# State-space layer: the out-projection weights are loaded at the top of each group, for the first group in the head

## The reference

```python
proj = hidden_states @ in_proj_w.T                     # 512 -> 8192 gate, 10240 xBC, 128 dt
xBC = silu(causal_conv(xBC, conv_w))                   # 4 taps
x, Bm, Cm = jnp.split(xBC, ...)                        # 128 heads of 64, 8 groups of B and C of 128
cs = jnp.cumsum(dt * A)                                # per head, chunks of 128
y = ssd(x, Bm, Cm, D, dt)                              # exp(cs_l - cs_s) * (C B^T), times x * dt
yg = y * silu(gate)
out = yg / sqrt(mean(yg**2 over the group) + eps)
return out @ out_proj_w.T                              # 8192 -> 512
```

## Time and profile before

| | |
|---|---|
| median of 3 runs | 2196.39 us (2195.48 to 2200.21) |
| profiled execution | 2204.72 us, of which the span 2202.9 us |
| PE busy | 2085.4 us (95%) |
| DVE, ACT, POOL busy | 1588.6, 1187.4, 817.5 us |
| mean granted TensorE clock | 0.991 |
| DMA moved | 285.39 MB |
| loads of the out-projection weights | 8, issued from 555.1 to 1852.7 us |

### The profile page before, as it was taken

One profiled execution on the slowest core, in us unless ns is written; L12 is line 12 of the kernel. 1 busy time (PEld: TensorE's weight loads), 2 busy tenths in 40 slices (PEclk: granted clock), 3 DMA queues, 4 the chain that ended last, 5 costly groups with the idle time before them and its releaser, 6 DMA issues. The chain is left out here.

```text
span 2202.9 us, 38224 instructions
## 1 busy us (share of the span) xinstructions
PE 2085.4 (95%) x11176; PEld 1572.1 (71%) x11176; DVE 1588.6 (72%) x3212; ACT 1187.4 (54%) x2858; POOL 817.5 (37%) x692
## 2 busy tenths in 40 slices
PE   7899899998999999999999999999999999989998
PEld 4555555547777877877877887787787787867877
DVE  4676666647886798589589678858958966967345
ACT  4554645315664576467367447647736845754330
POOL 4452424212443254245235325424523542553230
PEclk9999999999999999999999999999999999999999
DMA  6000000005989688687787958868788796812101
GB/s 245 20 17 1 1 1 1 15 1 145 234 218 193 159 202 172 116 217 189 121 207 198 172 149 197 179 116 221 191 125 203 195 167 154 197 57 87 48 10 39
DMA packets 243108, 285.39 MB, mean 130 GB/s; under 512 B 9424, under 2 KB 210896, under 8 KB 242256
## 3 DMA queue, kind: packets, MB, share of 16 engines
q1 hardware_dynamic: 242896, 282.86, 55.3%
HBM read 280.20 MB, written 103.02 MB: 174 GB/s over the span
## 5 line engine op out<-in xcount | busy, mean ns | idle before, releaser
L2024 PE MATMUL ab_ps<-xh_keep,wh 128*128 128x512 f32 x1148 | 456.7, 398 | 2.6 <-DVE yt L1765 1.9
L2026 PE MATMUL ab_ps<-xh_keep,wl 128*128 128x512 f32 x1148 | 448.0, 390 | 0.0
L2025 PE MATMUL ab_ps<-xl_keep,wh 128*128 128x512 f32 x1148 | 447.1, 389 | 0.0
L1718 DVE SCALAR_TENSOR_TENSOR xs<-ab_ps,par,xs 128x510 f32<-128x510 f32 (+2 forms) x384 | 284.6, 741 | 45.0 <-ACT xs L1385 31.6
L1604 POOL TENSOR_TENSOR wl<-raw_weights,wh 128x512 fp32r<-128x512 f32 x141 | 182.7, 1296 | 353.5 <-ACT wh L1364 351.8
L1746 DVE TENSOR_TENSOR decayed<-ab_ps,b_scores 128x384 f32<-128x384 f32 x512 | 266.9, 549 | 48.3 <-ACT ab_ps L1414 38.7
L1413 ACT ACTIVATE ab_ps<-rows,ncs 128x256 f32<-128x256 f32 x512 | 238.9, 467 | 97.4 <-DMA rows<-skewed_rows 65.7
L2024 PEld LDWEIGHTS ab_ps<-xh_keep,wh 128*128 128x128 f32 x1148 | 215.8, 188 | 49.3 <-issue 4.8
L2026 PEld LDWEIGHTS ab_ps<-xh_keep,wl 128*128 128x128 f32 x1148 | 215.5, 188 | 46.6
L2025 PEld LDWEIGHTS ab_ps<-xl_keep,wh 128*128 128x128 f32 x1148 | 216.0, 188 | 42.4
L1625 POOL TENSOR_TENSOR ssq<-ssq,sq 128x512 f32<-128x512 f32 x112 | 144.3, 1288 | 217.9 <-ACT sq L1422 217.9
(11 more groups left out here) (280 smaller groups left out, 4076.9 us busy)
## 6 DMA issues: line engine op xcount, KB each, us to landing
rows<-skewed_rows SPq DMA_DIRECT2D x252, 384.0 KB, 3.9
skewed_rows<-sum_rows SPq DMA_DIRECT2D x63, 1024.0 KB, 12.3
raw_weights<-win_dram SPq DMA_DIRECT2D x144, 256.0 KB, 8.6
skewed_rows<-sum_rows SPq DMA_DIRECT2D x63, 512.0 KB, 14.5
qkv_or_out_weights<-wout_dram SPq DMA_DIRECT2D x8, 2048.0 KB, 17.3
raw_weights<-wgu_dram SPq DMA_DIRECT2D x11, 512.0 KB, 3.5
w<-w_dram SPq DMA_DIRECT2D x1, 3584.0 KB, 17.8
draw<-wd_dram SPq DMA_DIRECT2D x1, 2816.0 KB, 9.5
```

The costliest lines, as they stand in the source:

```text
L1718: ins = nc.vector.scalar_tensor_tensor(y[:, :, back:], z[:, :, 0:SEQ - back], param(g, sub, TAPS - 1 - back), y[:, :, back:], ALU.mult, AL ...
L2024: nc.tensor.matmul(out, w_h, x_h, start=(k == 0), stop=False)
L2025: nc.tensor.matmul(out, w_h, x_l, start=False, stop=False)
L2026: last = nc.tensor.matmul(out, w_l, x_h, start=False, stop=(k == KT - 1))
```

## The change

The call that loads the out-projection weights leaves unit 1. For group 0 it now stands in the head, ahead of the store of the sums, behind a wait for `abs_done`. For each later group it stands at the group's top, ahead of the first slice.

```diff
             for n in range(3, 7):
                 load_in(0, n)
+            sp.wait_ge(abs_done, 2)
+            load_out(0)
             sp.wait_ge(sums_ready, 2)
             sp.dma_start(ssm["rows"][:, :, 0:SEQ], csT.rearrange("p (b s) -> p b s", s=SEQ)).then_inc(kept, 16)
...
                     more = g < LOOPS or 8 + 2 * j < SUBS
+                    if g and not j:
+                        load_out(g)
                     if more:
                         load_in(g, 8 + 2 * j)
-                    if j == 1:
-                        load_out(g)
                     load_rows(n + 1, 0)
```

## The result

The changed kernel takes 2180.85 us in the median of 6 runs (2175.83 to 2185.97), the kernel before 2198.3 in the median of its 6 (2193.59 to 2209.14). The ratio is 0.9927, 95% interval 0.9903 to 0.9951: faster by 0.73%. Forecast were 2168 us and a range of 2162 to 2180. The direction was right, the forecast gain (28.4 us) was larger by two thirds than the measured one (17.45 us), and the time lies 0.85 us above the range. The profiled execution took 2182.37 us, span 2180.5, against 2204.72 and 2202.9 before.

A forecast was written before the change was run, and what follows sets the result against it. The state-space loop was taken as TensorE-bound, with ScalarE waiting for row loads queued behind 2 MB of out weights. From the 2196.4 us median, 28.2 (groups 1 to 7) and 1.0 (group 0) off, one microsecond added: 2168, range 2162 to 2180.

The forecast's parts named there:

- the empty stretch of 15 us: Before groups 1 to 7, DMA engines nearly idle (group 2: 903 to 918), so the moved load costs nothing.
- the margin of 1.1 us: Group 2, unit 2: without the out weights ahead, the row load lands at 942.3, before ScalarE is due at 943.4.
- C: Groups 1 to 7: load was hidden anyway, another DMA ends the wait; half of 28.2 gained, 2182, or no change, 2196; chance 0.10.
- D: Group's top: the wait there blocks SyncE's queue, unit 1's row load lands 7.5 us late; 2205.7 us; chance 0.05.
- B: Head: the weights take 17 us there and group 0's chain carries the slip; 2179.5 us, milder from 2173; chance 0.08.
- the waits are the same work: Whole kernel: the gain read from the 2204.72 us profile is subtracted unchanged from the 2196.39 us median, 8.3 lower.
- The term of 28.2 us: Groups 1 to 7, units 1 and 2: seven stretches take 234.0 us against 205.8 undisturbed; all 28.2 taken back.
- The slack between ScalarE's wait and TensorE's loss: Group 2: ScalarE waits 7.4 us, TensorE loses 5.7, so some 2 us of wait cost nothing.
- the lower bound of 20 us: Groups 1 to 7: least gain, if a microsecond beyond the slack is missed in each group.
- 1.0 us back: Group 0: staging copy to row load takes 15.0 us, 15.95 with the out weights ahead; the head's slip is hidden.
- the 387 GB/s of the earlier trace: Out weights' rate before they landed in group 2; 2.1 MB need 5.4 us plus about 2, so 7.4.
- the one microsecond that the sum had allowed for missed margins: In the sum: added for groups missing the 1.1 us margin of unit 2's row load, 2167.2 to 2168.

The follow-up runs named there:

- the head alone: Against the kernel before: group 0 loads the out weights in the head, groups 1 to 7 in unit 1 as before; ratio 0.9992.
- the combination: Against the changed kernel: every group loads at its top, group 7's first staging copy issued at the end of group 6; 2171.11 us, ratio 0.9919 to before.

## Why the prediction was right or wrong

**The mechanism in groups 1 to 6 was right.** The 2 MB ahead of the row load were the wait (one slice in their place removes it), the empty stretch of 15 us took them without cost, the margin of 1.1 us for the row load of unit 2 was there (941.6 against 942.63), and no wait moved to unit 1. In all nine profiles of kernels with the load elsewhere, divided or cut, these groups stand at the floor. Rivals C and D are out. The measured 2180.85 lies near the numbers of B (2179.5) and C (2182), but by chance and not by their mechanisms: the 2 MB took 8.6 to 10.1 us in the head and not 17, and no row load was late in groups 1 to 6.

**The step that failed most** is the one from the profile to the median: "the waits are the same work, so I take the difference off as it is". They were not the same. The term of 28.2 us came from an execution that stood 8.3 us above the median of three (6.4 above that of all six). Within the pair of profiles the waits of groups 1 to 6 came back in full, 23.7 us, and the profiled execution of after stands only 1.5 us above its median: of the 12.9 us that the forecast was too low, 8.3 - 1.5 = 6.8 are this. The likely reason is that the profiled execution of before stood above its median because of these very waits: two other profiles of before lose 9.8 and 9.7 us in the same groups, and that of the head alone 10.7. To subtract the waits of a slow execution from the median of ordinary ones then counts their excess twice. That the ordinary runs beside the first profile had the smaller waits is not shown, since none of them was profiled. It may also be the chip: in the first pair, before and after, the 512 KB copies landed in 14.5 and 14.2 us and group 0 began at 550.8 and 550.7, where the eleven later profiles have 13.5 to 14.0 us and 552.5 to 556.1.

Two smaller readings beside it were off and moved nothing. The slack between ScalarE's wait and TensorE's loss was put at 2 us; in the second profile of before a wait of 5.01 us lengthens the stretch by 1.9, so it is about 3, which helps to explain why a quarter of the load goes unnoticed. And the lower bound of 20 us for groups 1 to 7 should by its own words be 28.2 less seven, 21.2.

**The second term mis-sized is group 7**, 4.5 of the 28.2 us. I read its unit 1 by its length, 33.9, which looked like the others, and not by its releaser: ScalarE stops there for 4.8 us with "issue" and waits for the transfer for 0.5 us only. The runs showed the stop with the 2 MB in unit 1, at the top, and with an eighth of them: 4.2 to 4.9 us, and 32.1 to 34.1 us for the two units, in eleven profiles. It falls to 2.4 us when the staging copy is not in flight.

**The third is group 0.** Forecast was 1.0 us back; in the first pair of profiles 1.3 us were lost. The step was the landing time of the 2 MB in the head: 7.4 us from the 387 GB/s of the earlier trace rows, measured 10.1 there, and 8.8 at the top of group 2. The rate itself was right, as the DMA columns of the changed kernel show at the top of group 2, where the load was issued at 902.34:

```profile
903.00:906.00 3.00, 3.00 (x15) 2.49 (x14) 0.90 (x2) 0.90 (x2) 0.00 (x0) 1.00 0.70 186
906.00:910.00 4.00, 4.00 (x19) 3.32 (x18) 4.00 (x7) 0.00 (x0) 0.00 (x0) 1.00 1.04 400
```

What the sum left out is the slow start, 186 GB/s in the first three microseconds, and the transfers that move beside the 2 MB: a slice of 256 KB in both places, and in the head the store too. The slip of the store was therefore 6.0 us and ran into the staging copy of unit 0. A formula of the Trainium skill ("DMA: Bandwidth & Descriptors", section "Anatomy of one DMA — SWDGE (gpsimd) path") would give 6.8 us for the 2 MB, an estimate; the page gives it for transfers that GpSimd issues, which the prediction did not say, and here SyncE issues them. The traces say 8.8 and 10.1, and they decide.

The collision depends on when the sums are ready, which differs between executions. In the first profile of the changed kernel the store is issued 2.1 us after the 2 MB and lands after 9.3 us; in the two others it is issued 5.5 and 5.0 us after them and lands after 5.3 and 5.8. Group 0 lasts 193.8 us in the first and 186.5 and 185.2 in the others.

6.8 + 4.5 + 2.3 for group 0, less the one microsecond that the sum had allowed for missed margins, is 12.6, against the 12.9 that are missing. This is the bookkeeping of one pair of profiles and their medians; it shows which terms differ, not why.

**What stays open.** The same group 0 took 185.2, 186.5 and 193.8 us in three profiles of the changed kernel, and 187.3, 189.9 and 192.5 in three of before. So single profiles cannot rank the places of the load in group 0 (186.5 and 186.9 at its top, 185.2 to 193.8 in the head, 187.3 to 192.5 in unit 1). The timed runs put the top 4.2 us ahead of unit 1; that the top is better than the head is likely from the order of the queue but not shown, since the combination, the one kernel with the load at the top of group 0 that was timed beside the change as given, differs in group 7 too. The moment at which group 0 begins also differs, by 5.4 us over the thirteen profiles (550.7 to 556.1), and was not looked into. Why the copies from device memory to device memory land within 13.6 us in one execution and 14.5 in another was not tried. That the stop with "issue" is the fetch of code is inferred from the packet of instructions that comes before each end of it, and from its length following the copy; the records do not say for which engine a packet is, and the fetch itself was not taken away.

## What to carry to other kernels

A large load that is not needed for long should not stand in a queue ahead of small ones that are needed at once; look for the stretch in which the DMA engines are idle and the buffer is already free. Before a wait seen in one profile is subtracted from a median, ask whether the profiled execution stands above the median, and whether that very wait is the reason; a second profile of the same kernel helps to answer it. And read each stall by what released it: a stretch of the same length can have another cause.

## What the runs showed of the hardware

A stall that is a little longer can cost more than its own length, through TensorE's clock. In the two later profiles of before, ScalarE's waits in unit 1 of groups 1 to 6 were 3.9 to 5.2 us; TensorE itself stood for 0.8 to 1.7 us, the two units lost 1.2 to 2.1 us, and the granted clock stayed 1.00. In groups 2 to 6 of the first profile the waits were 5.9 to 7.4 us and TensorE stood for 2.4 to 2.7 us. In four of these five groups the clock of the two units was 0.95 and they lost 4.1 to 5.7 us. Group 3 shows the fall, from full clock (2.4 GHz) to half (1.2 GHz), as TensorE begins again after standing for 2.37 us until 1145.73:

```profile
1145.00:1145.50 0.50, 0.00 (x0) 0.00 (x0) 0.50 (x2) 0.00 (x0) 0.50 (x1) 1.00 0.62 37
1146.00:1147.00 1.00, 1.00 (x8) 0.68 (x7) 1.00 (x3) 1.00 (x3) 0.19 (x1) 0.50 0.92 332
```

The length of the stall alone does not decide. In the fifth of these groups, group 5, TensorE stood for 2.65 us, longer than in group 3, the clock stayed 1.00, and the two units lost 3.5 us. In group 7 it stood for 2.1 to 2.9 us in the eleven profiles with the copy in flight: three keep 1.00 (stalls of 2.12, 2.43 and 2.85 us) and take 32.1 to 32.8 us for the two units, eight show 0.95 (stalls of 2.16 to 2.85 us) and take 33.4 to 34.1. The Trainium skill describes such a fall and its cost ("TensorE: Matmul & The Clock Gate", section "Part 1: The HAM clock gate"); the traces agree that the clock falls after a stall of TensorE, by the rows of group 3 above.

In group 7, which is written out behind the hardware loop, ScalarE stands for 4.2 to 4.9 us in the middle of its work while 1.5 MB of copies and the row loads occupy the DMA engines, and goes on 1.5 to 1.7 us after one packet of instructions has started on them. With the copy out of the way it is 2.4 us. The packets of instructions pass through the same DMA engines as the data (queues 14 and 1 in the DMA views); that the one waits behind the other is the likely cause, not a shown one.
